# The query-key mask of the first sixteen-head attention, laid into PSUM by sixteen 32x32 tiles of the array

## What is computed

```python
q = _split_heads(query @ Wq + bq, B)       # (16, 16 heads, 128, 8)
k = _split_heads(key @ Wk + bk, B)
v = _split_heads(value @ Wv + bv, B)
scores = jnp.einsum('bhqd,bhkd->bhqk', q, k) * scale
scores = jnp.where(mask == 0, NEG_INF, scores)
probs = jax.nn.softmax(scores, axis=-1)
attn = jnp.einsum('bhqk,bhkd->bhqd', probs, v)
return attn @ Wo + bo
```

## Time and profile before

| | |
|---|---|
| median of 3 runs | 1222.13 us (1221.99 to 1222.42) |
| profiled execution | 1221.81 us, span 1220.1 us |
| granted TensorE clock, mean | 0.973 |
| TensorE busy | 1116.6 us, 92% |
| VectorE busy | 767.4 us, 63% |
| ScalarE busy | 711.3 us, 58% |
| GpSimd busy | 410.7 us, 34% |

### The profile page before, as it was taken

The page is one execution under the profiler, slowest core; times in us unless marked ns, Lnnn a source line. Parts: engine busy times, 40 slices in busy tenths (PEclk is TensorE's granted clock), DMA queues, the critical chain, the costliest instruction groups (busy, mean ns, idle before and its releaser), DMA issues. The chain is left out here.

```text
span 1220.1 us, 24686 instructions
## 1 busy us (share of the span) xinstructions
PE 1116.6 (92%) x9741; PEld 835.1 (68%) x9757; DVE 767.4 (63%) x1577; ACT 711.3 (58%) x1303; POOL 410.7 (34%) x606
## 2 busy tenths in 40 slices
PE   1779799889999999999999889998969998999998
PEld 0568457878888888888887556664556764466667
DVE  5857656655565565566555149896468995745554
ACT  2569552156566666666666456777537877644440
POOL 0200001123323323443444353431464452644441
PEclk9979899999999999999999899999989999999999
DMA  4500000100000000000000000000000000033320
GB/s 178 207 1 1 1 1 1 71 1 1 1 2 1 2 1 1 2 2 2 1 1 2 1 1 2 2 2 2 1 1 2 2 2 1 5 89 101 91 85 19
DMA packets 13120, 27.09 MB, mean 22 GB/s; under 512 B 2608, under 2 KB 4944, under 8 KB 12112
## 3 DMA queue, kind: packets, MB, share of 16 engines
q1 hardware_dynamic: 13008, 25.54, 6.4%
HBM read 24.28 MB, written 1.25 MB: 21 GB/s over the span
## 5 line engine op out<-in xcount | busy, mean ns | idle before, releaser
L1294 POOL TENSOR_TENSOR work<-work 128x1024 f32<-128x1024 f32 x64 | 121.3, 1896 | 267.0 <-DVE work L1388 267.0
L1375 DVE TENSOR_REDUCE work<-psum 128x8 f32<-128x1024 f32 x64 | 78.0, 1219 | 86.5 <-PE psum L1174 86.5
L1316 ACT ACTIVATE work<-work 128x1024 f32<-128x1024 f32 x64 | 67.4, 1053 | 95.8 <-DVE work L1379 95.8
L1386 DVE TENSOR_REDUCE work<-work 128x8 f32<-128x1024 f32 x64 | 77.4, 1210 | 70.6 <-ACT work L1316 70.6
L1753 PEld LDWEIGHTS psum<-w_down,work 128*128 128x128 f32 x768 | 99.4, 191 | 28.8 <-issue 27.3
L1753 PE MATMUL psum<-w_down,work 128*128 128x128 f32 x768 | 100.6, 275 | 1.1 <-DVE x L1870 0.7
L1039 ACT ACTIVATE work<-psum 128x512 f32<-128x512 f32 x128 | 72.8, 596 | 46.2 <-PE psum L908 45.3
L1079 DVE TENSOR_REDUCE work<-psum 128x8 f32<-128x1024 f32 x64 | 75.2, 1217 | 22.0 <-PE psum L894 22.0
L908 PEld LDWEIGHTS psum<-ident,work 128*128 128x128 f32 x512 | 56.9, 142 | 44.4 <-ACT work L1036 21.8
L908 PE MATMUL psum<-ident,work 128*128 128x128 f32 x512 | 75.7, 281 | 7.5 <-ACT work L1039 5.9
L1379 DVE TENSOR_TENSOR work<-psum,work 128x1024 f32<-128x1024 f32 x64 | 78.4, 1225 | 6.4
(11 more groups left out here) (342 smaller groups left out, 2647.0 us busy)
## 6 DMA issues: line engine op xcount, KB each, us to landing
work<-chosen SPq DMA_DIRECT2D x80, 128.0 KB, 3.0
x<-in_x SPq DMA_DIRECT2D x1, 1024.0 KB, 4.8
ctx_tok<-in_ctx SPq DMA_DIRECT2D x1, 1024.0 KB, 6.8
ctxt<-in_ctxt SPq DMA_DIRECT2D x1, 1024.0 KB, 10.2
mask<-in_mask SPq DMA_DIRECT2D x1, 1024.0 KB, 7.1
w_down<-in_down SPq DMA_DIRECT2D x1, 1024.0 KB, 6.2
ctx_tok<-in_g SPq DMA_DIRECT2D x1, 1024.0 KB, 4.6
big<-in_u SPq DMA_DIRECT2D x1, 1024.0 KB, 7.4
```

What stands on the lines that cost most here:

```text
L1294: pool.tensor_tensor(prob[:, u % 2, h, :], prob[:, u % 2, h, :], rinv[:, u % 2, h].unsqueeze(2).broadcast_to([P, 8, P]), ALU.mult)\
L1316: act.activation(p, p, ACT.Exp).then_inc(S["exp"], 1)
L1375: dve.tensor_reduce(nmax[:, u % 2, h], s, AX.X, ALU.max, negate=True).then_inc(S["max"], 1)
L1386: dve.tensor_reduce(rsum[:, u % 2, h], prob[:, u % 2, h, :], AX.X, ALU.add).then_inc(S["sum"], 1)
```

## The change

Three more copies of the mask are made on chip, each turned round by 32, 64 or 96 partitions: row p of copy g is row (p + 32 g) mod 128 of the mask. They lie in the second half of `negb` and in the buffer of the integer mask, which has been read by then. SyncE makes them by six transfers from on-chip memory to on-chip memory once the mask is ready, and TensorE waits for them before the first scores. The mask matmul of bank g becomes four: tile r takes 32 rows of copy g and 32 columns of the identity, and puts the result on the partition group (r + g) mod 4 of bank g. Over the four banks the sixteen tiles use each of the sixteen 32x32 blocks of the array once. In a3 the matmuls stay what they were. `skip_group_check` is a flag for the simulator.

```diff
+    def turned_masks(self):
+        spare = self.mask2[:, :].bitcast(BF16)
+        return self.mask16, self.negb[:, T // 2:].bitcast(BF16), spare[:, 0:T], spare[:, T:]
+
+    def turn_full_mask(self, sp, set_up, turned):
+        sp.wait_ge(set_up, 1)
+        for g, to in enumerate(self.turned_masks()[1:], 1):
+            at = 32 * g
+            sp.dma_start(to[0:P - at, :], self.mask16[at:, :]).then_inc(turned, 16)
+            sp.dma_start(to[P - at:, :], self.mask16[0:at, :]).then_inc(turned, 16)
+
     def full_mask_rows(self, b, g):
-        return self.ident16[:, :], self.mask16[:, b * P:(b + 1) * P]
+        mask = self.turned_masks()[g]
+        for r in range(4):
+            of, to = slice(32 * r, 32 * r + 32), (r + g) % 4
+            yield slice(32 * to, 32 * to + 32), self.ident16[of, of], mask[of, b * P:(b + 1) * P]
...
     def key_mask_rows(self, b, g):
         r = slice(32 * g, 32 * g + 32)
-        return self.pick[r, b % 8, :], self.mask3[r, b // 8 * P:(b // 8 + 1) * P]
+        yield slice(0, P), self.pick[r, b % 8, :], self.mask3[r, b // 8 * P:(b // 8 + 1) * P]
...
                 for g in (2 * half, 2 * half + 1):
-                    lhs, rhs = mask_rows(b, g)
-                    pe.matmul(bank[g][:, :].rearrange("p (i c) -> p i c", i=4), lhs,
-                              rhs.unsqueeze(1).broadcast_to([rhs.shape[0], 4, P]),
-                              start=True, stop=False)
+                    for rows, lhs, rhs in mask_rows(b, g):
+                        pe.matmul(bank[g][rows, :].rearrange("p (i c) -> p i c", i=4), lhs,
+                                  rhs.unsqueeze(1).broadcast_to([rhs.shape[0], 4, P]),
+                                  start=True, stop=False, skip_group_check=True)
...
         pe.wait_ge(S["setup"], 1)
+        if turn_mask:
+            pe.wait_ge(S["rotated"], 96)
         score(0)
...
-    return Stage(tensor, scalar, vector, gpsimd, none, ready)
+    def sync(sp):
+        if turn_mask:
+            turn_mask(sp, S["setup"], S["rotated"])
+        yield
+        yield
+
+    return Stage(tensor, scalar, vector, gpsimd, sync, ready)
```

More of the change, by code:

```diff
@@ L231, in __init__ @@
         self.ready, self.added, self.over = ready, added, over
-def none(eng):
-    yield
-    yield
 def in_turn(programs):
@@ L822, in keep, with small_head_attention @@
         act.activation(self.k.xnt[:, n * w:(n + 1) * w], self.out[:, 0:w], ACT.Copy).then_inc(S["kept"], 1)
-def small_head_attention(k, prev, tag, sub, names, bias_q, bias_k, bv, bo, mask_rows, set_mask, weights_of, selectors):
+def small_head_attention(k, prev, tag, sub, names, bias_q, bias_k, bv, bo, mask_rows, set_mask, weights_of, selectors,
+                         turn_mask=None):
     nc, bank, psum = k.nc, k.bank, k.psum
@@ L844, in small_head_attention @@
     S = {n: k.sem(f"{tag}_" + n) for n in
-         ("setup", "stepped", "zero", "proj", "k", "q", "v", "km", "vp", "score", "max", "sub", "exp", "turn", "pt", "pv",
+         (*(("rotated",) if turn_mask else ()), "setup", "stepped", "zero", "proj", "k", "q", "v", "km", "vp", "score", "max", "sub", "exp", "turn", "pt", "pv",
           "inv", "on", "out", "added", "stated", "xb", "sel", "chain", "root", "normed", "turned", "kept")}
@@ L894, in score @@
                 mm = pe.matmul(bank[g][:, :], q[r, :], km[r, c, :, :].rearrange("p i c -> p (i c)"),
-                               start=False, stop=True)
+                               start=False, stop=True, skip_group_check=True)
             mm.then_inc(S["score"], 1)
@@ L2133, in a2 @@
                                             k.rows[:, R_BV2:R_BV2 + P], k.gated_bo[:, 0, :], k.full_mask_rows,
-                                            k.set_full_mask, 2, (8, 128))
+                                            k.set_full_mask, 2, (8, 128), k.turn_full_mask)
             def f2(prev):
```

## The result

| | before | after |
|---|---|---|
| median | 1222.13 us (5 runs, 1219.72 to 1224.06) | 1211.69 us (5 runs, 1211.26 to 1215.40) |
| profiled execution, span | 1221.81, 1220.1 | 1211.29, 1209.6 |
| granted TensorE clock, mean | 0.973 | 0.983 |

The ratio is 0.9922, 95% interval 0.9902 to 0.9942: 9.5 us less, between 7.1 and 12.0. The prediction had 6.6 us less and a range whose low end was 1214.0.

A forecast was written before the change was run, and what follows sets the result against it. TensorE was taken to bound a2, with VectorE close behind. Saving 6.3 us in the sequences plus 0.3 at b = 0 and b = 1 gave 6.6, so 1222.1 becomes 1215.5 us; range 1214.0 to 1222.3.

The forecast's parts named there:

- What bounds the kernel: In a2 TensorE is the bound, busy 105.6 of 112.3 us, with VectorE close behind at 95.0.
- The saving per sequence: In a2 the mask group shrinks from 0.97 to 0.43 us on TensorE, saving 0.54 us a sequence (bounds 0.21 and 0.66).
- L: Time from the first mask tile's start to the last one's on TensorE, taken as 0.12 us.
- The rule of 25 ns between starts: Skill rule on TensorE starts; would make L 0.38 and the saving 0.28 us a sequence, 3.4 us in all.
- The ceiling by each sequence's own wait: In a2 a sequence gains at most VectorE's present wait in it: 6.3 us summed, 7.7 the ceiling.
- VectorE's other wait: VectorE's normalisation, beside mask and scores, ends 1.47 us after the first mask start, scores 1.50: nearly late, not late.
- b = 0 and b = 1: First two sequences of a2, only the mask's second half on the chain: together 0.3 us saved, bounds 0 and 0.5.
- The copies: Six transfers under f1, landed by about 692 us, 20 us to spare: cost 0, bounds 0 and +0.5 us.
- A: Row groups cannot write one bank at once, so mask tiles go one at a time: slower, 1252 us; chance 0.10.
- B: No gain: the four banks' mask groups run one after another, saving 0, time 1222.1 us; chance 0.13 with similar cases.
- C: VectorE takes all: L near 0, saving 0.65 us or so a sequence, 1214.4 us; short end of the main case.
- D: A shift of the half-clock stretches, or dearer loads: a little slower, +3 to +6 us; chance 0.03.

The follow-up runs named there:

- one copy: The change with one turned copy instead of three, so that two banks share eight array blocks; 1216.70 us against 1222.82 for the kernel before, ratio 0.9946.
- diagonal tiles: Sixteen tiles as in the change, but all from the one mask on four diagonal blocks, no copies; 1221.35 us against 1221.12 for the kernel before, ratio 1.0006.

## Why the prediction was wrong, and what of it held

**What bounds the kernel.** Right: TensorE's chain through a2, with VectorE close behind.

**The saving per sequence.** The formula (0.66 - L, with 0.31 us behind the last start) gives 0.61 for the L of 0.05 that the trace shows, and 0.61 is what the chain shows. L was mis-sized: 0.12 was taken, from the gather's pace of loads on the same rows. The rows of a3 held instead, 0.004 to 0.006 us between starts. This term was worth 0.07 us in each of nine sequences, 0.6 us. (The eight loads in that row belong to four matmuls: a float32 matmul other than a transpose leaves two loads and two matmuls in this trace, as the eight for the four of the scores. A gather is 32 matmuls of the program with 64 records, not 64 matmuls.) The rule of 25 ns between starts, weighed in the prediction (the Trainium skill, TensorE: Matmul & The Clock Gate, "Wait — 56ns, not 53.3ns?"), did not hold for tiles on separate blocks, which start 0.004 us apart. Another section of the same page of the Trainium skill (Part 3: Packing small matmuls — row/col tiling) gives about 4 ns per tile, and with that the trace agrees.

**The ceiling by each sequence's own wait.** In a2 this is the step that failed most. "That saving counts only as far as VectorE waits now", taken sequence by sequence, gives 9 x 0.61 + 3 x 0.46 = 6.9 us with the right L; measured for these fourteen sequences were 0.80 + 6.98 = 7.8. About 0.2 of the 0.80 us at b = 2 is clock: 0.97 granted between 724 and 730 us instead of 0.88. The other 0.7 us lie in the steady stretch, for which the rule gives 6.3.

Two errors lie in it, and the runs without a mask and with one copy show both. First, the waits listed are not all of VectorE's slack: a period less its wait was 6.58 us before (6.81 in two of the thirteen) and is 6.49 without a mask. Of the 8.6 us that fell away with the mask, 1.6 stood in no listed wait. Second, a gain beyond a sequence's own wait is not lost. TensorE comes early with the scores of a short period, VectorE takes them late, and in the next, longer period VectorE has less to wait for. The period ending at 757.12 us was shortened by 0.80 us though TensorE saves 0.61 in it.

The rule that fits is: scores ready after TensorE's period less the saving, VectorE at least 6.50 us a period, the lead handed on. Worked out over the thirteen periods before (7.30, 7.23, 6.58, 7.29, 7.57, 7.23, 7.05, 7.29, 7.57, 7.23, 7.05, 6.58, 7.04), it gives 7.3, 5.2 and 8.5 us for the steady stretch in the change, with one copy and without a mask; measured were 7.0, 5.1 and 8.6. Without handing on it would give 6.7, 4.8 and 8.3, too little each time. The 0.3 us too much in the change come from a limit of the lead. Banks 2 and 3 may be filled only after VectorE's last subtraction, so the group at 748.59 takes 0.61 us instead of 0.36, and of TensorE's lead of 0.53 us 0.28 is left. With the lead held to 0.28 us the rule gives 7.0 in the change and 5.2 with one copy. The prediction had read the 6.49 us of the earlier trace rows and not used it: 93.0 - 13 x 6.49 = 8.6 was the ceiling.

**VectorE's other wait.** Right where TensorE still sets the period: for the maximum at 763.99 us the normalisation ends at 763.83 and the scores at 763.92. Elsewhere it is VectorE's own work, without a wait, that sets it.

**b = 0 and b = 1.** 0.3 was forecast, 0.25 measured, 0.20 and 0.05. At b = 1 the eight tiles took 0.62 us at the low clock, where they took 0.41 with the clock at 1.00 in the runs with nine matmuls added. a2's end gave 0.17 more, which the prediction did not have; that the last output product no longer waits so long behind TensorE's work is a likely reason, not shown.

**The copies.** Right: nothing, landed more than 20 us ahead of need.

**What was left out of the sum and the range.** The medians differ by 10.4 us and the ratio says 9.5, but a2 gives 8.2. The rest lies outside a2, a term that the sum put at nothing. Of the 2.9 us between the forecast and the ratio's 9.5, then, 0.6 are L, 0.7 the ceiling, 0.2 the clock at b = 2, 0.1 the two ends of a2, and 1.3 lie outside a2. Outside a2 the low-clock stretches fall differently from execution to execution; the kernel before ranged from 1219.6 to 1228.4 us over the series. The prediction took the three close runs it had (1221.99 to 1222.42) for the scatter and gave its low end 0.4 us of room. With the right terms for a2 the sum would have been 1213.9, itself 0.1 us under the range, and a range honest about that scatter 1211 to 1222. The ratios make it likely that part of the rest is a mean effect of the change; its cause stays open.

**Rivals.** A (one tile at a time on a bank) is refuted: in the change and with diagonal tiles four row groups write one bank within 0.02 us. The rule of the Trainium skill behind it (TensorEngine Tiling (Array Packing), Gotcha 1: PSUM Pressure: different row tiles cannot access one bank at the same time) does not show here, where the row groups write different partitions of the bank; the same partitions at once were not tried. B (banks in turn) is what happens when the blocks are shared, and not otherwise. C, VectorE as the new bound, was underpriced at 0.65 us a sequence as the most that could come. D had a shift of the low-clock stretches only as a loss of 3 to 6 us; the parts outside a2 differed by up to 6.2 us between two profiles of one kernel, and the change's own three profiles had a gain there and not a loss.

## What to carry to other kernels

Small tiles of the array run side by side only if each has a block of its own: four blocks used four times cost the same as four whole matmuls, and a copy that turns the data by 32 partitions is worth its transfers where they lie under earlier work. When a faster engine meets a second one close behind, don't cap the gain sequence by sequence with the waits listed; take the second engine's own period from a stage where it is the bound, and let leads carry over. Compare the clock over several executions before giving a range its width.

## What the runs showed of the hardware that was not expected

Sixteen 32x32 tiles of 512 bfloat16 columns start within 0.05 us, and the scores behind them, on 32 rows and 128 columns of the array each, start 0.36 us after the first of them; the same sixteen on four blocks need 0.97 us. The low level of the clock before b = 1 comes with TensorE's idle time of 2.6 us: with that filled down to 0.7 us the clock stayed at 1.00 from 720 to 730 us in two runs, and the scores of b = 1 took 1.14 us instead of 2.09. With an idle time of 2.2 us left, behind ten added matmuls, it was 0.50 from 726 to 728 us. Two executions of one kernel differed by 6.2 us in stretches where the program had not changed, with the granted clock at 0.973 and 0.964 on the mean.
